# Clearing semaphores beside the next stage, filling PE's waits with products of the identity, and issuing four peak products together

## What is computed

```
layer 0: cross attention, 1 head   | self attention, 16 heads, relative positions | 8 experts, top 2
layer 1: cross attention, 16 x 64  | gated delta rule                             | experts with capacity, slots
layer 2: cross attention, 16 x 16  | self attention with rotary tables            | experts with capacity, tokens
layer 3: cross attention, 16 x 16  | state space scan (conv, softplus, scan)      | experts, swiglu
```

```
q = LN(x) Wq;  k, v = [LN(ctx), LN(x)] Wkv;  out = softmax(q k^T / 8) v;  x = x + out Wout
```

## Time and profile before

| | |
|---|---|
| median of three runs | 3854.11 us (3847.34 to 3861.64) |
| profiled execution | 3848.74 us |
| its span | 3846.7 us, 55282 instructions |
| granted clock, mean | 0.925 of 2.4 GHz |
| busy in the span | PE 3324.0, DVE 2274.3, ACT 1509.4, POOL 902.6 us |

### The profile page before, as it was taken

How to read it: one execution, slowest core, us unless ns; L and a number is a source line. 1 busy time by engine, 2 the same in 40 slices (tenths; PEclk the granted TensorE clock), 3 DMA queues, 4 the chain that set the end, 5 groups by cost and what they waited for, 6 DMA issues and landing times. The chain is left out here.

```text
span 3846.7 us, 55282 instructions
## 1 busy us (share of the span) xinstructions
PE 3324.0 (86%) x20968; PEld 2026.2 (53%) x20968; DVE 2274.3 (59%) x3668; ACT 1509.4 (39%) x2233; POOL 902.6 (23%) x666
## 2 busy tenths in 40 slices
PE   8978796999999999999669597999875789995659
PEld 5835494665665656656436474444443444442225
DVE  4335214565664655655388305999562389974964
ACT  2335111423324334234256231667551147773311
POOL 1042001425425245254237102000020300000520
PEclk9979898999999999999889698999987889997879
DMA  5258462000001000000486326656101566620010
GB/s 199 83 168 271 178 240 78 7 6 4 7 1 56 9 4 6 6 1 1 98 310 230 137 113 179 129 117 132 29 15 41 178 161 130 132 47 21 0 46 34
DMA packets 228854, 346.75 MB, mean 90 GB/s; under 512 B 104176, under 2 KB 177584, under 8 KB 223984
## 3 DMA queue, kind: packets, MB, share of 16 engines
q1 hardware_dynamic: 228208, 342.16, 30.9%
q0 software_dynamic: 384, 1.05, 0.1%
HBM read 257.15 MB, written 86.02 MB: 89 GB/s over the span
## 5 line engine op out<-in xcount | busy, mean ns | idle before, releaser
L1585 DVE TENSOR_REDUCE L1x_pk<-L1x_psm 128x1 f32<-128x512 f32 (+1 forms) x576 | 374.9, 661 | 177.7 <-PE L1x_psm L1414 175.4
L1384 POOL TENSOR_TENSOR L1x_acc<-L1x_acc,L1x_pr 128x512 f32<-128x512 f32 x256 | 416.0, 1625 | 137.7 <-ACT L1x_pr L1561 119.3
L1561 ACT ACTIVATE L1x_pr<-L1x_pss 128x1024 f32<-128x1024 f32 x272 | 278.4, 1024 | 288.2 <-PE L1x_pss L1473 280.5
L1607 DVE TENSOR_TENSOR L1x_acc<-L1x_acc,L1x_pr 128x512 f32<-128x512 f32 x256 | 261.1, 1020 | 202.0 <-ACT L1x_pr L1561 197.6
L1193 DVE TENSOR_REDUCE L3x_pk<-L3x_psm 128x1 f32<-128x512 f32 x512 | 329.1, 686 | 36.2 <-PE L3x_psm L1027 30.0
L1193 DVE TENSOR_REDUCE L2x_pk<-L2x_psm 128x1 f32<-128x512 f32 x512 | 329.0, 686 | 31.7 <-PE L2x_psm L1027 25.9
L1170 ACT ACTIVATE L3x_pr<-L3x_pss 128x1024 f32<-128x1024 f32 x256 | 248.1, 1021 | 106.7 <-PE L3x_pss L1068 106.4
L1170 ACT ACTIVATE L2x_pr<-L2x_pss 128x1024 f32<-128x1024 f32 x256 | 248.1, 1021 | 103.2 <-PE L2x_pss L1068 102.9
L1473 PE MATMUL L1x_pss<-L1x_Q,L1x_K 64*128 64x256 f32 x2176 | 279.3, 376 | 0.0
L1439 PE MATMUL L1x_pss<-L1x_w,L1x_cT 128*128 128x256 f32 x1088 | 278.4, 380 | 0.0
L1434 PE MATMUL L1x_pss<-L1x_cT,L1x_w 128*128 128x512 f32 (+1 forms) x576 | 277.9, 573 | 0.0
(11 more groups left out here) (662 smaller groups left out, 5798.0 us busy)
## 6 DMA issues: line engine op xcount, KB each, us to landing
f0e_wt<-in_f_pieces SPq DMA_DIRECT2D x10, 3072.0 KB, 11.2
offset_rows<-s_rows SPq DMA_DIRECT2D x32, 768.0 KB, 5.3
L2x_KS<-L2x_key_parts SPq DMA_DIRECT2D x24, 1024.0 KB, 13.1
L3x_KS<-L3x_key_parts SPq DMA_DIRECT2D x24, 1024.0 KB, 13.0
s_add<-offset_rows SPq DMA_DIRECT2D x32, 512.0 KB, 7.4
n_cT<-in_ctxT SPq DMA_DIRECT2D x32, 512.0 KB, 4.8
f1e_wt<-in_f_pieces SPq DMA_DIRECT2D x8, 2048.0 KB, 13.7
L2x_key_parts<-n_kst SPq DMA_DIRECT2D x32, 384.0 KB, 2.9
```

What stands on the lines that cost most here:

```text
L1384: i = nc.gpsimd.tensor_tensor(acc[:, n, 1, :, :], acc[:, n, 1, :, :], pr[:, A % RING, :, 1, :], ALU.add)
L1561: nc.scalar.activation(pr[:, A % RING, :, :, :].rearrange("p h e q -> p (h e q)"), pss[:, x:x + 2, :].rearrange("p h n -> p (h n)"), ACT.E ...
L1585: nc.vector.reduce_max(pk[:, m, hq, j:j + 1], psm[:, i % 2, 0:NQ[j][1]], AX).then_inc(peak_read, 1)
L1607: i = nc.vector.tensor_tensor(acc[:, n, 0, :, :], acc[:, n, 0, :, :], pr[:, A % RING, :, 0, :], ALU.add)
```

## The change

Three things, and a small one.

1. **Semaphore numbers.** Stage names take their numbers from one of two fixed rows of 38 numbers, in turn, and lasting semaphores from the numbers above them. At a stage's end there is the block's barrier alone (POOL drains ahead of it), and POOL clears the stage's numbers behind it, with no other barrier; the next stage uses the other row. Lasting semaphores are cleared once, at the program's end. The stage inside the loop over batches (`repeated=True`) keeps one barrier with its clear. The program as built has 58 barriers at stage ends and 57 clears.

2. **Products of the identity.** `keep_busy(nc, k, room, n)` issues n f32 products of the 128 x 128 identity with itself into a PSUM tile that nothing reads. It stands where PE has nothing to do: at the start of every layer norm (11, in two of them 14 and 22) and behind its transposes (2), at the start of latent attention's pass (20) and at its end (9), in the routers, in the rotary stage, at the start of the experts, in layer 0's self attention (14 at the start, 2 ahead of the early row products, 10 ahead of the scores of pair 12, 8 at the end), in the context attentions of layers 2 and 3, the scan and some more. The built program has 541 of them.

3. **Four peak products at once.** Queries are cast to bf16 without zeros (`Qb`). For each m and j there are four products of 64 rows each: two heads side by side for each qt, into `psm[:, 0:2]` (qt 0) and `pss[:, 2:4]` (qt 1). DVE reduces two banks in one instruction, 1024 columns to two. So tiles go through two banks of `pss` instead of four, and there are 18 such quads a group, about one to two tiles, at a tile's end.

4. LAG in relative self attention is 4 instead of 3.

```diff
 @contextmanager
-def stage(nc, *names, also=()):
+def stage(nc, *names, repeated=False):
+    numbers = NUMBERS["now"]
+    row = numbers.rows[numbers.stages % 2]
+    numbers.stages += 1
     with ExitStack() as held:
-        sems = [held.enter_context(nc.semaphore(n)) for n in names]
+        sems = [held.enter_context(nc.semaphore(n, num=row[i])) for i, n in enumerate(names)]
         with nc.Block(no_gpsimd_drain=True) as block:
             yield (block, *sems)
-        numbers = sorted(s.num for s in (*sems, *also))
-        starts = [n for n in numbers if n - 1 not in numbers]
-        runs = [range(n, next(m for m in range(n, n + len(numbers) + 1) if m not in numbers)) for n in starts]
-
-        for run in runs:
-            nc.all_engine_barrier(sems_to_clear=run)
+
+            @block.gpsimd
+            def _(pool):
+                pool.drain()
+        used = range(row[0], row[0] + len(names))
+        if repeated:
+            nc.all_engine_barrier(sems_to_clear=used)
+        else:
+            nc.gpsimd.sem_clear(used)
...
+def keep_busy(nc, k, room, n):
+    for _ in range(n):
+        nc.tensor.matmul(room, k.ident[:, :], k.ident[:, :], start=True, stop=True, skip_group_check=True)
...
         @block.tensor
         def _(pe):
+            keep_busy(nc, k, spare[:, :], idle)
             if dstT is not None:
...
                     m.then_inc(turned, 1)
+                keep_busy(nc, k, spare[:, :], 2)
...
-    PART = NB * 4
-    PEAKS = KC * PART
-    QEV = 3 * KC
+    PEAKS = KC * NB
+    QEV = 2 * KC
...
                     def peak_products(g, first, last):
                         for i in range(first, last):
-                            m, j, hq = peak_of(i)
-                            h, qt = divmod(hq, 2)
+                            m, j = divmod(i, NB)
                             o, w_ = NQ[j]
                             if i == 0:
                                 pe.wait_ge(q_ev, QEV * (g + 1))
-                            if hq == 0:
-                                pe.wait_ge(k_cast, NK * g + m * NB + j + 1)
-                            if i == 1 and g >= 1:
-                                pe.wait_ge(o_done, KC * g)
-                            if i >= 2:
-                                pe.wait_ge(peak_read, PEAKS * g + i - 1)
-                            nc.tensor.matmul(psm[:, i % 2, 0:w_], qzb[:, g % 2, m, h, qt * P:(qt + 1) * P], Kb[:, m, o:o + w_],
-                                             start=True, stop=True).then_inc(peaks, 1)
+                                if g >= 1:
+                                    pe.wait_ge(o_done, KC * g)
+                                    pe.wait_ge(exps, ALL * g)
+                            pe.wait_ge(k_cast, NK * g + i + 1)
+                            if i >= 1:
+                                pe.wait_ge(peak_read, QT * (PEAKS * g + i))
+                            for qt in range(QT):
+                                for h in range(2):
+                                    half = slice(64 * h, 64 * h + 64)
+                                    p = nc.tensor.matmul(peak_banks(qt)[:, h, 0:w_], Qb[half, g % 2, m, qt * P:(qt + 1) * P], Kb[half, m, o:o + w_],
+                                                         start=True, stop=True)
+                                p.then_inc(peaks, 1)
...
-                        x, done = n % 4, peaks_by(n - 1)
+                        x, done = n % 2, peaks_by(n - 1)
...
-    LAG = 3 if relative else 0
+    LAG = 4 if relative else 0
...
+                    if 0 < p < LAG or p == 0 and x:
+                        keep_busy(nc, k, pst[:, 0, 0, 0, :], 2)
...
+                keep_busy(nc, k, pst[:, 0, 0, 0, :], 14 if relative else 6)
...
+                    if relative and s == PAIRS - LAG:
+                        pe.wait_ge(rel_act, 4 * PAIRS)
+                        pe.wait_ge(rel_dve, 4 * PAIRS)
+                        keep_busy(nc, k, psr[:, 0, 0:P], 10)
```

More of the change, by code:

```diff
@@ L256, in project_residual @@
 def project_residual(nc, k, srcT, w, name, chunks=KC, bias=None, held=None):
-    with Tensors(nc) as t, stage(nc, name + "_load", name + "_mm", name + "_sum", also=() if held is None else (held.here,)) as (block, load, mm, summed):
+    with Tensors(nc) as t, stage(nc, name + "_load", name + "_mm", name + "_sum") as (block, load, mm, summed):
         wt = t.sb(name + "_w", [P, chunks, D]) if held is None else held.w
@@ L1968, in layer0_ff @@
                  "s_down s_added t_mm t_act t_hid t_down y_ev y_out").split()
-        with stage(nc, *[name + "_" + n for n in names], also=(small, cleared, k.moved, k.back, *s_here)) as (block, *sems):
+        with stage(nc, *[name + "_" + n for n in names]) as (block, *sems):
             (routed, ranked, chain, shifted, exped, choices, slots, tiles, x_in0, x_in1, turned, turn_ev, t_here0, t_here1, t_here2, s_mm, s_act, s_hid,
@@ L2505, in layer2_ff @@
         names = "marked weighted gath gath_act gath_dve up_mm hid down_mm y_ev turned turn_ev out_mm".split()
-        with stage(nc, *[name + "_" + n for n in names], also=(loaded.here, *pieces, small)) as (block, *sems):
+        with stage(nc, *[name + "_" + n for n in names]) as (block, *sems):
             (marked, weighted, gath, gath_act, gath_dve, up_mm, hid, down_mm, y_ev, turned, turn_ev, out_mm) = sems
@@ L2695, in latent_projections @@
 def latent_projections(nc, k, d, pre, held, qT, kT, V, fetch=None):
-    with Tensors(nc) as t, stage(nc, pre + "qk_mm", pre + "v_mm", also=held.loads) as (block, qk_mm, v_mm):
+    with Tensors(nc) as t, stage(nc, pre + "qk_mm", pre + "v_mm") as (block, qk_mm, v_mm):
         loads = held.loads
@@ L3085, in rotate @@
 def rotate(nc, k, held, both, name):
-    with Tensors(nc) as t, stage(nc, name + "_mm", name + "_a", name + "_b", also=(held.here,)) as (block, mm, ca, cb):
+    with Tensors(nc) as t, stage(nc, name + "_mm", name + "_a", name + "_b") as (block, mm, ca, cb):
         load, rot, tab = held.here, held.rot, held.tab
@@ L3148, in layer2_self @@
         layer_norm(nc, k, k.X, k.N, "s2m", k.NT, gain=d["s2_g2"], shift=d["s2_h2"])
[L3149 removed]
+        with stage(nc, "s2_b2_unused", "s2_b2_unused1") as (block, _u, _v):
             @block.vector
@@ L3575, in layer1_self @@
         O = t.sb("d_O", [P, TT, D])
-        with Tensors(nc) as u, stage(nc, "g_turned", "g_copied", "g_chain", "g_root", also=(nw_load,)) as (block, turned, copied, chain, root):
+        with Tensors(nc) as u, stage(nc, "g_turned", "g_copied", "g_chain", "g_root") as (block, turned, copied, chain, root):
             sqr = u.sb("g_sq", [P, TT, D])
@@ L3918, in _ @@
                 sp.wait_ge(stored, 16)
+    numbers = NUMBERS["now"].all
+    nc.all_engine_barrier(sems_to_clear=range(numbers[0], numbers[-1] + 1))
 def layouts(inp):
```

114 lines of the change are left out of this document (71 added, 43 removed).

## The result

| | before | after |
|---|---|---|
| median, us | 3850.7 (4 runs, 3843.2 to 3861.6) | 3737.2 (4 runs, 3734.2 to 3748.4) |
| profiled execution, us | 3848.7 | 3736.9 |
| its span, us | 3846.7 | 3735.1 |
| mean granted clock | 0.925 | 0.962 |

The ratio is 0.9703, 95% interval 0.9673 to 0.9734. The profiled executions lie 111.8 us apart, where 119 were forecast.

A forecast was written before the change was run, and what follows sets the result against it. TensorE bounds the kernel, with time lost between stages and at half clock. Stage ends 60, peak products 2, s0 12 and identity products 45 sum to 119: 3848.7 to 3730 us, range 3672 to 3790 for 8 in 10.

The forecast's parts named there:

- Stage ends, 60 us: At stage ends, 148 fewer barriers at 0.41 us each save 60 us, bounds 37 and 62.
- The floor (0.10): Rival, chance 0.1: branching sets a floor of 0.74 us at stage ends, so 37 us saved instead of 60; 3753.
- it is itself two steps of 0.41, so nothing fixed stands beside the barriers: Stage ends: the 0.74 us gap with two barriers is all barrier price, within a tenth, so the full 60 us is taken.
- Four peak products, 2 us: Latent attention's quads: 6.6 us won, 10.6 lost to new waits, 6 of old waits gone; 2 us saved, bounds -12 and 45.
- The 6 us for the waits of before: Latent attention: of 26.2 us of present waits for reduces, in 72 places, 6 us counted as real and saved.
- s0, 12 us: Layer 0's relative attention: 9 us from full clock in twelve early steps, 12 in all with LAG 4; bounds 0 and 18.
- The wait that was to shrink to 2 or 3 us: Near the end of s0's attention, PE's 5.03 us wait for the shifted rows shrinks to 2 or 3.
- Identity products, 45 us besides s0's 9: Identity products filling PE's waits keep its clock at 2.4 GHz in stretches behind them: 45 us saved, bounds 15 and 75.
- I take half: 45 us: In 25 half-clock stretches PE is busy 180.56 us; full clock would save 90, and half of that is taken.
- overruns of 6: Identity products outlasting their wait where the clock is low at stage start: about 2 us each in L1na, f1n and s2i.
- Clock not held (0.15): Rival, chance 0.15: transposes and barriers behind the identity products let the clock fall, so 45 us becomes 0; 3775.
- Slower (0.02): Rival, chance 0.02: identity products run at 1.2 GHz ahead of real work, 120 us extra, 3895; decides from 74 us of overrun.

The follow-up runs named there:

- only_numbers: Changed kernel with the semaphore rows alone (old peak code, LAG 3, no identity products): 3779.3 us, ratio 0.9816 to the kernel before.
- no_fill: Changed kernel without any of its 570 identity products, all else kept: 3774.7 us, ratio 0.9805 to the kernel before.
- lag3: Changed kernel with LAG 3 instead of 4 in s0's relative attention, identity products kept: 3734.3 us, ratio 0.9708 to the kernel before.
- again: The changed kernel unedited, measured once more later: 3738.5 us, ratio 0.9719 to the kernel before.
- The trims: Three versions of the changed kernel with fewer identity products, mainly where they ran past their wait: 3724.4, 3722.2 and 3718.8 us.
- numbers_back: Changed kernel with the earlier stage ends: 147 clearing barriers behind the blocks' barriers, each clearing all the stage's numbers: 3824.6 us, ratio 0.9937 to the kernel before.
- transposed_twice: Changed kernel with two transposes of the identity in place of each identity product: 3732.7 us, ratio 0.9703 to the kernel before.

## Why the prediction was right

**Stage ends, 60 us.** Right: 62 (stage ends) to 63 (span) by the trace of only_numbers, 64 to 77 by its medians. The floor (0.10) is gone with the step behind s2p: 0.34 where it would have been 0.74. The step "it is itself two steps of 0.41, so nothing fixed stands beside the barriers" held; what is left at a stage end, 0.32 to 0.34, is the block's own barrier.

**Four peak products, 2 us.** Right, for the reasons given. The sub-terms that can be read stand: 0.22 in, 0.10 out (0.14 was taken), 24 waits with 9.9 us. By the group period it is 7 rather than 2, mostly because the way out is 0.04 cheaper in 128 quads. The 6 us for the waits of before were a guess, and no run shows them by themselves; with the measured prices some 4 or 5 are left for them. The period fell by 0.88, within the 1.5 that was said. The medians give 1.5 to 2.8, which is not to be told from nothing.

**s0, 12 us.** 194.4 to 182.4, 12.0. But the split was wrong: no_fill shows 11.0 of it from identity products, where I had 9, and lag3 1.6 in the stage for LAG and nothing in the whole, where I had 3. The wait that was to shrink to 2 or 3 us is 0.47.

**Identity products, 45 us besides s0's 9.** This is the term that was mis-sized: 37.5 in all, so 26.5 besides s0's 11, within the bounds of 15 and 75. The step that failed is "I take half: 45 us", with overruns of 6 already in it, which makes 51 of gains. Outside s0 the stages gained 47 and lost 20; by the trace of "again" they gained 41 and lost 13. So the gains were 4 to 10 short. The overruns were 10 and 5, not far from 6, but not where they had been put: s2i cost 2.7 (1.1 in "again") and L1na with L1nb 1.7 (1.1), f1n 0.5, f2n 1.4 (0.5), and the first two stages 3.4 (2.2), which the prediction doesn't name. The other 8 to 10 us of losses stand mostly in L2x, L3x and the scan's last stage, and their cause is open. The trims say that the overruns may have cost more than these stages show. That a product which warms PE early can lengthen the wait behind it, and lose the clock there, was in no rival.

**Clock not held (0.15).** Falls: 0.962 granted against 0.928 without the products. Transposes were thought to be its cause, and hold and raise the clock themselves. **Slower (0.02).** Falls: identity products do overrun, but 74 us would have been needed, and the stages show 20 of losses at most.

**Sum.** 60 + 2 + 12 + 45 = 119 against 112 in profiled executions. By the runs the terms are 63 to 71, 2 to 7, 12 and 26.5, together 103 to 117: the identity products brought some 18 less than forecast, and stage ends and peak products 3 to 16 more, so part of the agreement is luck. That the medians of only_numbers are 10 better than its term and numbers_back's 86 worse than 60 (12 of these are the experiment's own) shows that a sum of parts is good to about 10 to 20 us here. I had treated gap length and clock as separate terms, and L3xp shows that they are not.

## What to carry over

- A barrier of all engines cost 0.33 to 0.41 us in each stage end here, and at L3xp PE ran slower behind a long gap made of them, even with identity products ahead of it. Clear semaphores on one engine beside the next stage, from alternating rows, so that a stage ends with one.
- Work that only holds TensorE's clock should be sized to the wait at half clock as well as at full; where it outlasts the other engines of its stage, it lengthens the stage, as in s2i. Count for each place when the other engines are done; 66 products less made the kernel 20 us faster here, though the stages concerned show only 6 to 8 of it. Where the wait behind the next group is for a load, speeding up the group ahead of it may only move the idle time, as in the first stages.
- Try such parts together as well as apart: short gaps and filled waits did more together at L3xp than either alone.

## What the runs showed of the hardware

- Transposes of f32 hold the granted clock as products do, if they cover the same time: 0.960 and 0.962. They also raise it from half to full by themselves (L1na in transposed_twice).
- At the very start PE ran at half speed: in no_fill the products at 11.36 take 6.34 us, the same number at 18.48 takes 3.70. Those of the changed kernel take 3.67 from the first, behind identity products. The trace's first clock entry stands at 16.74 in no_fill and at 10.12 in the changed kernel; a window ahead of it reads 1.00 only because nothing is recorded there.
- A plain barrier cost 0.33 to 0.38 us at a stage end, one with a clear behind it 0.41.
- A change of the array's shape from 128*128 to 64*128 cost 0.22 us, and the way back 0.10.
